# A fused attention and FFN kernel: down projections and one 128x128 product as three split products, the last layernorm's factor from VectorE

## Chip, cores and metric

The kernel runs on one core of a Trainium2 chip. The metric is the device time of one execution in microseconds (us), the median of several runs. The core has five engines that work side by side, each through its own instructions in order: TensorE (PE in the profile; PEld is its weight load), VectorE (DVE), ScalarE (ACT), GpSimd (POOL) and SyncE (SP, here only DMAs). They wait for each other through counting semaphores.

## What is computed

The input x has 4 batches of 2048 tokens with 256 features, all in fp32. The reference, cut to what matters:

```python
x = x + attn_a(layernorm(x))        # 16 heads of 16, linear attention
x = x + ffn(layernorm(x))
x = x + attn_b(layernorm(x))        # only the first 16 tokens of a batch differ from "+ ob"
x = x + ffn(layernorm(x))

# attn_a: feature map elu(.) + 1 on q and k
q, k, v = fm(x @ Wq + bq), fm(x @ Wk + bk), x @ Wv + bv
kv  = einsum('bkhd,bkhm->bhdm', k, v)
out = einsum('bqhd,bhdm->bqhm', q, kv) / max(einsum('bqhd,bkhd->bqh', q, k), 1e-6)
out = out.reshape(B, S, D) @ Wo + bo

# ffn: square(relu(x @ Ws1)) @ Ws2 + routed experts, whose weights are truncated to 0 or 1
```

The routed experts count only where a token's second logit reaches its first; the kernel tests a bound on that once and skips them, as in these runs. The third sublayer adds the row ob to all tokens except the first 16 of each batch, 64 in all, which get a chain of small products of their own.

## The kernel before

The tokens are worked in 16 groups of 512 (4 tiles of 128 tokens). All of x and all q stay in SBUF.

The first pass, 0 to about 180 us, makes k, q and the sums k^T x for each group; the change leaves its instructions alone. Its products q and k are split already: a matrix is written as hi + lo, where hi is the value rounded to the type float32r (a copy by ScalarE) and lo the rounded rest (a subtraction), and a product is hi*hi + hi*lo + lo*hi, three matmuls in that type, summed in PSUM.

The second pass is a loop over steps i = 0 to 17, three stages deep. Step i works on group i for attention, on group r = i - 1 for the first FFN (F1, F2), and on group v = i - 2 for the last FFN's down projection (F4). The order on each engine is that of its `step` function, written by hand:

- TensorE: transposes of x for group r (L1367, into PA); the attention product of group i (L1377, into PT and PB), which waits until VectorE has emptied PB (L998); `down(PA)` for group v (L1356); slot 1; the up product for group r (L1395, into PT); transposes of o_tok (L1403, into PB); four transposes that spread ln_rsq of the second layernorm over the partitions, called r2 (L1408, into PT); slot 2; the output product W of group i, three split products (L1425, L1426, L1431); the product of h2s with wc (L1435), which adds to the up product; slot 3; `down(PB)` for group r (L1356).
- ScalarE: copies the transposes of x (L688), scales half of F4's result (L695), rounds o to o_hi (L702), then relu (L706) and square (L708) of h2, and behind L1435 relu (L714) and square (L716) of h3.
- VectorE: quotients (L945, L949) and o_tok (L953), half of F4's result (L969), slot 1, o_lo (L977), h2s = h2 times the spread factor (L984), slot 2, adds W to x (L990), statistics (L934), adds F2 to x (L998), slot 3, statistics (L934) for the last layernorm.
- GpSimd: `rsq`, once for each of the two layernorms: five small instructions for the variance (L454 to L461) and a power -1 (L463), then adds the row ob to x (L429), slot 1, adds y3, the half of F4's result that ScalarE scaled (L517), slot 2.

The scale enters the FFN as relu(x*w)^2 times rstd^2, so the factor is 1/variance (times a constant that is folded in). wc is ws2 times w1c, so that the last FFN's hidden layer comes from the same PSUM bank. The slots hold the pieces of the chain for the 64 tokens (`chain(i, slot)`), different in each step. The down projections, the product with wc and the up product are plain fp32 matmuls, two instructions each on TensorE.

Of the kernel before, what the change touches and what calls it, by code (L numbers as in the profile page):

```python
# [44 lines left out]
def hybrid_kernel(nc, x_in, Wq, bq, Wk, bk, Wv, bv, Wo, bo, qw, qb, kw, vw, vb, ow, ob,  # L45
# [18 lines left out]
    with ExitStack() as ctx:  # L64
# [78 lines left out]
        squares = o_tok.rearrange("p k n -> p (k n)").rearrange("p (c n) -> p c n", c=C)  # L143


        with ExitStack() as pass1_memory:
            def sb1(name, shape):
                return pass1_memory.enter_context(nc.sbuf_tensor(name, shape, F32R))

            wq_hi, wq_lo = sb1("wq_hi", [P, C, D]), sb1("wq_lo", [P, C, D])  # L150
            wk_hi, wk_lo = sb1("wk_hi", [P, C, D]), sb1("wk_lo", [P, C, D])
            xt_hi, xt_lo = sb1("xt_hi", [P, C, GT]), sb1("xt_lo", [P, C, GT])
# [107 lines left out]
        (c_wts, c_vecs, c_xs, c_out, c_blk, c_bd, c_bd_sb, c_brow, c_brow_sb, c_fold, c_fold_sb, c_stat, c_rstd, c_z, c_zt, c_zt_sb,  # L260
         c_qkv, c_lin, c_k, c_vi, c_ss, c_rs, c_lt, c_q1, c_kn, c_knt, c_knm, c_vsel, c_vm, c_logit, c_lg, c_pr, c_pt, c_p1,
         c_inv, c_pv, c_o, c_ot, c_ot_sb, c_ql, c_dsum, c_diff, c_flag, c_proj, c_hid, c_relu, c_sq, c_ffn, c_added, c_final, c_zero,
         c_pool) = [sem(f"c_{n}") for n in (
             "wts", "vecs", "xs", "out", "blk", "bd", "bd_sb", "brow", "brow_sb", "fold", "fold_sb", "stat", "rstd", "z", "zt", "zt_sb",
             "qkv", "lin", "k", "vi", "ss", "rs", "lt", "q1", "kn", "knt", "knm", "vsel", "vm", "logit", "lg", "pr", "pt", "p1",
             "inv", "pv", "o", "ot", "ot_sb", "ql", "dsum", "diff", "flag", "proj", "hid", "relu", "sq", "ffn", "added", "final", "zero",
             "pool")]

# [1332 lines left out]
```

## Time and profile before

| | |
|---|---|
| median of 3 runs | 457.89 us (457.2 to 458.69) |
| profiled execution | 457.29 us, of it span 455.5 us |
| mean granted TensorE clock | 0.993 |
| busy: PE | 425.2 us (93%) |
| busy: DVE | 293.2 us (64%) |
| busy: ACT | 183.8 us (40%) |
| busy: POOL | 203.5 us (45%) |
| chain that ended last | PE 82%, DVE 7%, ACT 5%, POOL 2% |
| from 194 to 443 us | PE 238.8 of 249 us busy, DVE 185.7, ACT 90.9, POOL 132.6 |

The span reaches from the first to the last instruction; the profiled execution's time has 1.8 us around it. "Busy" counts the time in which an engine works on an instruction. Matmuls overlap each other, so a matmul's own duration is longer than the distance from one to the next. The chain follows the work that ended last back from the end, at each step to what it waited for. Line numbers are those of the kernel before; a helper's line stands for all its calls.

### The profile page before, as it was taken

What the parts mean: (1) busy time and instruction counts of PE and PEld (TensorE: products, weight loads), DVE (VectorE), ACT (ScalarE), POOL (GpSimd) and SP (SyncE); (2) the same over time, 40 slices, a digit from 0 to 9 for tenths busy, and PEclk for the clock granted to TensorE, in tenths of its full rate; (3) what the DMA queues carried; (4) which work ended last, traced back from release to release, by engine and by line L of the source; (5) the groups of instructions that cost most, each with busy time, mean ns of one, the idle gap of its engine ahead of it and who ended that gap; (6) DMA issues with size and microseconds to landing.
All of it is one profiled execution on the core that took longest, in us unless ns stands there. A gap on an engine that the chain in (4) does not pass through costs nothing.

```text
span 455.5 us, 7618 instructions
## 1 busy us (share of the span) xinstructions
PE 425.2 (93%) x2570; PEld 354.7 (78%) x2570; DVE 293.2 (64%) x651; ACT 183.8 (40%) x321; POOL 203.5 (45%) x334
## 2 busy tenths in 40 slices
PE   7799989999999999688979999999999999999971
PEld 4689979998898999676858876878777787787851
DVE  4565575455556543459637697878858777887843
ACT  2464545555455541224134532333243323424440
POOL 3344442433334350036144367566527527635562
PEclk9999999999999999999999999999999999999997
DMA  8512111111100003100110111011010111011102
GB/s 260 179 48 78 63 47 46 48 46 46 46 0 1 0 2 89 8 2 3 51 46 4 50 49 35 15 48 47 4 47 1 50 48 35 16 49 47 48 32 71
DMA packets 22776, 20.58 MB, mean 45 GB/s; under 512 B 3255, under 2 KB 22717, under 8 KB 22717
## 3 DMA queue, kind: packets, MB, share of 16 engines
q1 hardware_dynamic: 22156, 19.32, 13.5%
q8 instruction: 30, 0.49, 0.4%
q10 hardware_dynamic: 560, 0.52, 0.4%
q14 instruction: 30, 0.24, 0.2%
HBM read 11.32 MB, written 8.45 MB: 43 GB/s over the span
## 4 chain that ended last, share of the span: by engine, by line
PE 82%; DVE 7%; ACT 5%; issue 2%; POOL 2%; DMA 1%; POOLq 0%; ACTq 0%; DVEq 0%
PE PG L1236 11%; PE PB L1356 6%; PE PT L1395 6%; PE PA L1356 5%; PE PB L1377 5%; PE PA L1425 4%; PE PA L1431 3%; PE PA L1426 3%; PE PA L1226 3%; PE PA L1227 3%; PE PA L1228 3%; PE PB L1214 3%; PE PB L1212 3%; PE PB L1213 3%; PE PT L1435 3%; PE PA L1367 3%
## 5 line engine op out<-in xcount | busy, mean ns | idle before, releaser
L454 POOL TENSOR_TENSOR ln_a<-ln_bn 128x4 f32<-128x4 f32 x32 | 6.5, 205 | 132.0 <-DVE ln_bn L934 132.0
L1236 PE MATMUL PG<-scratch 128*128 128x256 f32 x256 | 58.0, 379 | 1.3 <-DVE scratch L821 1.3
L821 DVE SCALAR_TENSOR_TENSOR scratch<-scratch,PB 128x1024 f32<-128x1024 f32 x16 | 19.5, 1221 | 60.3 <-ACT scratch L570 60.3
L1236 PEld LDWEIGHTS PG<-scratch 128*128 128x128 f32 x256 | 47.4, 190 | 7.4 <-issue 1.5
L535 ACT ACTIVATE scratch<-x_all,ln_shift,ln_rstd 128x255 f32 (+1 forms) x60 | 31.1, 589 | 36.7 <-PE PG L1236 30.2
L934 DVE BATCH_NORM_STATS2 ln_bn<-x_all 128x6 f32<-128x256 f32 x128 | 44.9, 413 | 0.9
L416 POOL TENSOR_SCALAR ln_rstd<-ln_mv 128x4 f32<-128x4 f32 x16 | 3.7, 228 | 91.3 <-DVE ln_mv L743 88.4
L1212 PE MATMUL PB<-wk_hi,xt_hi 128*128 128x256 f32 x128 | 39.0, 305 | 0.4 <-DVE xt_lo L768 0.4
L429 POOL TENSOR_TENSOR x_all<-x_all,scratch 128x1024 f32 (+1 forms) x16 | 38.2, 2388 | 0.6 <-ACT scratch L535 0.5
L429 POOL TENSOR_TENSOR x_all<-x_all,ob_rows 128x1024 f32<-128x1024 f32 x16 | 37.8, 2360 | 0.0
L695 ACT ACTIVATE scratch<-PA,ln_rsq 128x256 f32<-128x256 f32 x32 | 13.4, 471 | 59.3 <-PE PA L1356 35.4
L1425 PE MATMUL PA<-wo_hi,o_hi 128*128 128x256 f32 x128 | 33.5, 295 | 3.1 <-ACT o_hi L702 2.7
L1214 PE MATMUL PB<-wk_hi,xt_lo 128*128 128x256 f32 x128 | 36.2, 282 | 0.0
L1213 PE MATMUL PB<-wk_lo,xt_hi 128*128 128x256 f32 x128 | 36.1, 282 | 0.0
L463 POOL TENSOR_TENSOR ln_rsq<-ln_a,minus_ones 128x4 f32<-128x4 f32 x32 | 32.5, 1015 | 2.5
L1356 PE MATMUL PA<-ws,scratch 128*128 128x256 f32 x128 | 30.4, 380 | 2.7 <-ACT scratch L688 2.7
L990 DVE TENSOR_TENSOR x_all<-PA,x_all 128x1024 f32<-128x1024 f32 x16 | 19.6, 1225 | 20.6 <-PE PA L1431 20.6
L977 DVE TENSOR_TENSOR o_lo<-PB,o_hi 128x512 fp32r<-128x512 f32 x32 | 20.6, 684 | 18.6 <-ACT o_hi L702 18.5
L1426 PE MATMUL PA<-wo_lo,o_hi 128*128 128x256 f32 x128 | 31.9, 282 | 0.0
L1356 PE MATMUL PB<-ws,scratch 128*128 128x256 f32 x128 | 31.1, 386 | 0.0
L1395 PE MATMUL PT<-scratch 128*128 128x512 f32 x64 | 30.9, 605 | 0.0
L576 ACT ACTIVATE scratch<-PA,minus_one 128x1024 f32<-128x1024 f32 x16 | 17.8, 1115 | 30.2 <-PE PA L1228 28.9
(239 smaller groups left out, 1039.0 us busy)
## 6 DMA issues: line engine op xcount, KB each, us to landing
out_dram<-x_all SPq DMA_DIRECT2D x16, 512.0 KB, 3.1
x_all<-n_L_attn_a_inputs_q_dram SPq DMA_DIRECT2D x15, 512.0 KB, 3.6
x_all<-n_L_attn_a_inputs_q_dram ACTq DMA_DIRECT2D x2, 128.0 KB, 2.8
x_all<-n_L_attn_a_inputs_q_dram SPq DMA_DIRECT2D x2, 128.0 KB, 2.6
scratch<-in_L_attn_a_Wk_dram SPq DMA_DIRECT2D x1, 256.0 KB, 4.6
scratch<-in_L_attn_a_Wq_dram ACTq DMA_DIRECT2D x1, 256.0 KB, 5.0
scratch<-in_L_attn_a_Wv_dram SPq DMA_DIRECT2D x1, 256.0 KB, 6.8
scratch<-in_L_attn_a_Wo_dram SPq DMA_DIRECT2D x1, 256.0 KB, 6.2
```

What stands on the lines that cost most here:

```text
L429: nc.gpsimd.tensor_tensor(x_group(n), x_group(n), rows_[:, :].rearrange("p (o d) -> p o d", o=1).to_broadcast([P, T, D]), ALU.add).then_in ...
L463: nc.gpsimd.tensor_tensor(ln_rsq[:, slot, :], a, minus_ones[:, :], ALU.pow).then_inc(done, 1)
L535: nc.scalar.activation(dst[:, t:t + 1, 0:width], x_tile(n, t)[:, :, 0:width], ACT.Identity, scale=ln_rstd[:, slot, t:t + 1], bias=ln_shift ...
L934: nc.vector.bn_stats(ln_bn[:, slot, t:t + 1, :], x_tile(n, t)).then_inc(bn, 1)
L1212: mm(dst, hi, wk_hi[:, c, :], start=(c == 0), stop=False)
L1213: mm(dst, hi, wk_lo[:, c, :], start=False, stop=False)
L1214: last = mm(dst, lo, wk_hi[:, c, :], start=False, stop=(c == C - 1))
L1236: last = mm(PG[:, c, 0:D], k_tok[:, t, c * P:(c + 1) * P], xn[g % 2][:, t, :], start=(g == 0 and t == 0), stop=(g == G - 1 and t == T - 1))
L1356: last = mm(four(pair)[:, t, :], h[:, t * P:(t + 1) * P], ws2[:, :], start=True, stop=True)
L1395: last = mm(PT[:, 0, :], w1c[:, c, :], x2t[:, c, :], start=(c == 0), stop=(c == C - 1))
L1425: mm(four(PA)[:, t, :], hi, wo_hi[:, c, :], start=(c == 0), stop=False)
L1426: mm(four(PA)[:, t, :], hi, wo_lo[:, c, :], start=False, stop=False)
```

## The change

Four parts:

1. `down` takes hi and lo of the hidden layer and of ws2 and makes three matmuls for each tile of 128 tokens. The product with wc becomes three matmuls of 512 columns; the third, with h2_lo, has a wait of its own. ws2 and wc are split once, in `fold_ffn` (ScalarE) and in step 0 (VectorE).
2. For this the hidden layers are needed as hi and lo. ScalarE squares twice, first into h2_hi (h3_hi), rounded, then in place; GpSimd subtracts (`h2_low`, `h3_low`). The factor now multiplies before the square, so it is 1/sqrt(variance) (power -0.5, in `half_rstd2`) and h2 stands for what h2s was.
3. The last layernorm's factor is VectorE's reciprocal (`reciprocal_variances`), placed after the quotients and ahead of the writes of o_tok; GpSimd makes only the variances (`four_variances`). VectorE's statistics for it stand ahead of slot 3.
4. Buffers lie elsewhere in SBUF; several semaphores of the chain for the 64 tokens are joined into three that count on (c_once, c_made, c_taken).

```diff
-            def rsq(slot, j, bn, powed, done):
+            def four_variances(slot, j, bn, powed):
...
-                nc.gpsimd.tensor_tensor(ln_rsq[:, slot, :], a, minus_ones[:, :], ALU.pow).then_inc(done, 1)
+            def half_rstd2(r):
+                ge(pool, r2_mm, r)
+                four_variances(0, r, bn2, pow2)
+                pool.wait_ge(pow2, 5 * r + 5)
+                nc.gpsimd.tensor_tensor(ln_rsq[:, 0, :], ln_a[:, 0, :], minus_half[:, 0:T], ALU.pow).then_inc(rsq2, 1)
+            def h2_low(r):
+                pool.wait_ge(f1_sq, r + 1)
+                ge(pool, f2_mm, r)
+                nc.gpsimd.tensor_tensor(h2_lo[:, :], h2, h2_hi[:, :].bitcast(F32), ALU.subtract).then_inc(h2_lo_done, 1)
+            def h3_low(v):
+                pool.wait_ge(f3_sq, v + 1)
+                ge(pool, f4_mm, v)
+                nc.gpsimd.tensor_tensor(h3_lo[:, :], h3, h3_hi[:, :].bitcast(F32), ALU.subtract).then_inc(h3_lo_done, 1)
...
 # ScalarE, step
-                    ge(act, f1_scaled, r)
+                    ge(act, h2_lo_done, r)
                     nc.scalar.activation(h2, PT[:, 0, :], ACT.Relu, scale=2.0).then_inc(f1_relu, 1)
-                    act.wait_ge(f1_relu, r + 1)
+                    act.wait_ge(f1_scaled, r + 1)
+                    ge(act, f2_mm, r)
+                    nc.scalar.activation(h2_hi[:, :], h2, ACT.Square).then_inc(h2_hi_done, 1)
+                    act.wait_ge(h2_hi_done, r + 1)
                     nc.scalar.activation(h2, h2, ACT.Square).then_inc(f1_sq, 1)
...
 # VectorE, step
+            def reciprocal_variances(v):
+                dve.wait_ge(pow3, 5 * (v + 1))
+                ge(dve, f4_scaled, 2 * v)
+                nc.vector.reciprocal(ln_rsq[:, 1, :], ln_a[:, 1, :]).then_inc(rsq3, 1)
...
                     nc.vector.reciprocal(norm_inv[:, :, :], norm_sb[:, :, :]).then_inc(o_norm, 1)
+                    if runs(v):
+                        reciprocal_variances(v)
...
-                    dve.wait_ge(f1_sq, r + 1)
+                    dve.wait_ge(f1_relu, r + 1)
                     dve.wait_ge(r2_mm, r + 1)
-                    nc.vector.tensor_tensor(h2s, h2, PT[:, 1, :], ALU.mult).then_inc(f1_scaled, 1)
+                    nc.vector.tensor_tensor(h2, h2, PT[:, 1, :], ALU.mult).then_inc(f1_scaled, 1)
...
 # TensorE
-            def down(pair, h, done):
+            def down(pair, hi, lo, done):
                 for t in range(T):
-                    last = mm(four(pair)[:, t, :], h[:, t * P:(t + 1) * P], ws2[:, :], start=True, stop=True)
+                    dst, tile = four(pair)[:, t, :], slice(t * P, (t + 1) * P)
+                    mm(dst, hi[:, tile], ws2_hi[:, :], start=True, stop=False)
+                    mm(dst, hi[:, tile], ws2_lo[:, :], start=False, stop=False)
+                    last = mm(dst, lo[:, tile], ws2_hi[:, :], start=False, stop=True)
...
-                    pe.wait_ge(f1_scaled, r + 1)
-                    mm(PT[:, 0, :], wc, h2s, start=False, stop=True, skip_group_check=True).then_inc(f3_mm, 1)
+                    pe.wait_ge(h2_hi_done, r + 1)
+                    mm(PT[:, 0, :], wc_hi[:, :], h2_hi[:, :], start=False, stop=False, skip_group_check=True)
+                    mm(PT[:, 0, :], wc_lo[:, :], h2_hi[:, :], start=False, stop=False, skip_group_check=True)
+                    pe.wait_ge(h2_lo_done, r + 1)
+                    mm(PT[:, 0, :], wc_hi[:, :], h2_lo[:, :], start=False, stop=True, skip_group_check=True).then_inc(f3_mm, 1)
```

GpSimd's queue in step 15, before; first the variance and power of the second layernorm (waiting for bn2; only its last row stands here), then those of the last (bn3).

```order
L463 TENSOR_TENSOR ln_rsq<-ln_a,minus_ones 128x4 [waits pow2]
L454 TENSOR_TENSOR ln_a<-ln_bn 128x4 [waits bn3,f4_scaled,out_dve]
L455 TENSOR_TENSOR ln_d<-ln_bn 128x4
L457 TENSOR_SCALAR ln_a<-ln_a 128x4 [waits pow3]
L459 TENSOR_TENSOR ln_d<-ln_d 128x4 [waits pow3]
L461 TENSOR_TENSOR ln_a<-ln_a,ln_d 128x4 [waits pow3]
L463 TENSOR_TENSOR ln_rsq<-ln_a,minus_ones 128x4 [waits pow3]
L429 TENSOR_TENSOR x_all<-x_all,ob_rows 128x1024 [waits t2_mm]
L517 TENSOR_TENSOR x_all<-x_all,scratch 128x512 [waits f4_scaled]
```

GpSimd's queue in step 15, now; h_lo is h2_lo or h3_lo, scratch beside h_hi is h2 or h3.

```order
L498 TENSOR_TENSOR h_lo<-scratch,h_hi 128x512 [waits f4_mm,f3_sq]
L475 TENSOR_TENSOR ln_a<-ln_bn 128x4 [waits bn2,r2_mm]
...
L488 TENSOR_TENSOR ln_rsq<-ln_a,minus_half 128x4 [waits pow2]
L475 TENSOR_TENSOR ln_a<-ln_bn 128x4 [waits bn3,rsq3]
L476 TENSOR_TENSOR ln_d<-ln_bn 128x4
L478 TENSOR_SCALAR ln_a<-ln_a 128x4 [waits pow3]
L480 TENSOR_TENSOR ln_d<-ln_d 128x4 [waits pow3]
L482 TENSOR_TENSOR ln_a<-ln_a,ln_d 128x4 [waits pow3]
L450 TENSOR_TENSOR x_all<-x_all,ob_rows 128x1024 [waits t2_mm]
L551 TENSOR_TENSOR x_all<-x_all,scratch 128x512 [waits f4_scaled]
L493 TENSOR_TENSOR h_lo<-scratch,h_hi 128x512 [waits f2_mm,f1_sq]
```

A subtraction stands at the head of the step and another at its end, ahead of what slots 1 and 2 hold in other steps; the second power is gone.

TensorE's queue in step 15 from the up product to the output product, before.

```order
L1395 MATMUL PT<-scratch 128x512 [waits t2_done]
L1403 MATMUL PB<-ident,scratch 128x128 [waits o_done]
L1403 MATMUL PB<-ident,scratch 128x128 x7
L1408 MATMUL PT<-ident,ln_rsq 128x128 [waits rsq2]
L1408 MATMUL PT<-ident,ln_rsq 128x128 x3
L1443 MATMUL PG<-ident,b_weights 128x64 [waits c_z]
L1443 MATMUL PG<-ident,b_weights 128x64
L1425 MATMUL PA<-wo_hi,o_hi 128x256 [waits f4_scaled,out_dve,o_hi_done]
```

The same stretch now.

```order
L1456 MATMUL PT<-scratch,ffn_weights 128x512 [waits t2_done]
L1463 MATMUL PT<-ident,ln_rsq 128x128 [waits o_done,rsq2]
L1463 MATMUL PT<-ident,ln_rsq 128x128 x3
L1471 MATMUL PB<-ident,scratch 128x128 [waits o_done]
L1471 MATMUL PB<-ident,scratch 128x128 x7
L1509 MATMUL PG<-ident,b_weights 128x64 [waits c_z]
L1509 MATMUL PG<-ident,b_weights 128x64
L1488 MATMUL PA<-wo_hi,o_hi 128x256 [waits f4_scaled,out_dve,o_hi_done]
```

The transposes of the factor (r2) stand ahead of those of o_tok and wait for the first write of o_tok besides, since that write frees their bank.

## Rows read from the trace of the kernel before

**Rows 1.** The chain of waits, 416 to 431 us: start, us, what.
```profile
416.61 0.86 PE PT L1435 x2
...
422.17 1.73 PE PA L1356 x8
...
423.90 1.72 PE PT L1395 x4
...
426.15 0.40 ACT o_hi L702
...
426.64 0.60 ACT o_hi L702
...
427.90 0.12 PE PA L1426
```

**Rows 2.** TensorE's timeline: start, us, line, out<-in; last matmuls of W, and L1435.
```profile
192.08 0.64 PE L1431 MATMUL PA<-wo_hi,o_lo 128*128 128x256 f32 x4
...
416.45 1.02 PE L1435 MATMUL PT<-scratch 128*128 128x512 f32 x2
...
430.25 1.02 PE L1435 MATMUL PT<-scratch 128*128 128x512 f32 x2
```

**Rows 3.** ScalarE's timeline in step 15.
```profile
417.51 0.69 ACT L714 ACTIVATE scratch<-PT,w1ob 128x512 f32<-128x512 f32 x1 [3.50 <-PE PT L1435]
...
418.23 0.63 ACT L716 ACTIVATE scratch<-scratch 128x512 f32<-128x512 f32 x1
...
426.15 1.08 ACT L702 ACTIVATE o_hi<-PB 128x512 fp32r<-128x512 f32 x2 [0.87 <-PE PB L1403]
...
427.12 0.61 ACT L706 ACTIVATE scratch<-PT 128x512 f32<-128x512 f32 x1
```

**Rows 4.** TensorE's timeline in the first pass: split products of 512 columns.
```profile
174.31 0.40 PE L1227 MATMUL PA<-xt_lo,wq_hi 128*128 128x512 f32 x1
...
174.55 0.39 PE L1228 MATMUL PA<-xt_hi,wq_lo 128*128 128x512 f32 x1
```

**Rows 5.** GpSimd's timeline in step 15.
```profile
422.07 0.20 POOL L454 TENSOR_TENSOR ln_a<-ln_bn 128x4 f32<-128x4 f32 x1 [0.31 <-DVE ln_bn L934]
...
423.34 1.01 POOL L463 TENSOR_TENSOR ln_rsq<-ln_a,minus_ones 128x4 f32<-128x4 f32 x1
...
424.32 2.36 POOL L429 TENSOR_TENSOR x_all<-x_all,ob_rows 128x1024 f32<-128x1024 f32 x1
...
426.64 1.33 POOL L517 TENSOR_TENSOR x_all<-x_all,scratch 128x512 f32<-128x512 f32 x1
```

**Rows 6.** VectorE's timeline in step 15.
```profile
422.60 0.55 DVE L949 RECIPROCAL norm_inv<-norm_sb 128x64 f32<-128x64 f32 x1
...
423.19 0.42 DVE L953 TENSOR_TENSOR scratch<-PT,norm_inv 128x256 f32<-128x256 f32 x1
...
424.46 0.88 DVE L969 SCALAR_TENSOR_TENSOR x_all<-PA,ln_rsq,x_all 128x256 f32<-128x256 f32 x2
...
425.25 1.57 DVE L1145 TENSOR_SCALAR b_weights<-q_all 64x256 f32<-64x256 f32 x1
...
426.78 1.29 DVE L977 TENSOR_TENSOR o_lo<-PB,o_hi 128x512 fp32r<-128x512 f32 x2
...
428.43 0.69 DVE L984 TENSOR_TENSOR scratch<-scratch,PT 128x512 f32<-128x512 f32 x1 [0.36 <-ACT scratch L708]
```

**Rows 7.** Step 5: VectorE's zz (L1070), then GpSimd's power for it.
```profile
269.31 1.18 DVE L1070 TENSOR_SCALAR b_weights<-q_all 64x256 f32<-64x256 f32 x1
...
267.96 0.55 POOL L478 TENSOR_TENSOR q_all<-q_all,minus_half 64x1 f32<-64x1 f32 x1
```

**Rows 8.** Step 7: VectorE's L1082 and L1083, then GpSimd's addition beside them.
```profile
296.64 1.69 DVE L1082 TENSOR_TENSOR q_all<-q_all,b_weights 64x256 f32<-64x256 f32 x1
...
298.36 0.42 DVE L1083 TENSOR_TENSOR q_all<-q_all 64x256 f32<-64x256 f32 x1
...
295.70 2.35 POOL L429 TENSOR_TENSOR x_all<-x_all,ob_rows 128x1024 f32<-128x1024 f32 x1
```

More of the change, by code:

```diff
@@ L138, in hybrid_kernel @@
+        wc_hi, wc_lo = sb("wc_hi", [P, F], F32R), sb("wc_lo", [P, F], F32R)
+        ws2_hi, ws2_lo = sb("ws2_hi", [P, D], F32R), sb("ws2_lo", [P, D], F32R)
+        h2_hi, h2_lo = sb("h2_hi", [P, GT], F32R), sb("h2_lo", [P, GT], F32R)
+        h3_hi, h3_lo = sb("h3_hi", [P, GT], F32R), sb("h3_lo", [P, GT], F32R)
+        part = parts(sb("ffn_weights", [P, 2560])[:, :])
         w1c = part(C * F).rearrange("p (c f) -> p c f", c=C)
@@ L142, in hybrid_kernel @@
         ob_t = part(C * P).rearrange("p (c n) -> p c n", c=C)
[L143 to L152, printed above, removed]
+        h2s = h2
         b_weights = sb("b_weights", [P, 2, 4, C * D])
@@ L259, in hybrid_kernel @@
         c_link = sem("c_link")
[L260 to L267, printed above, removed]
+        c_wts, c_vecs, c_xs, c_out, c_blk, c_bd, c_brow, c_fold, c_fold_sb, c_stat = [sem(f"c_{n}") for n in (
+            "wts", "vecs", "xs", "out", "blk", "bd", "brow", "fold", "fold_sb", "stat")]
+        c_rstd, c_z, c_zt, c_zt_sb, c_lin, c_ss, c_rs, c_lt, c_q1, c_knm = [sem(f"c_{n}") for n in (
+            "rstd", "z", "zt", "zt_sb", "lin", "ss", "rs", "lt", "q1", "knm")]
+        c_vm, c_logit, c_lg, c_pr, c_pt, c_p1, c_inv, c_pv, c_o, c_ot = [sem(f"c_{n}") for n in (
+            "vm", "logit", "lg", "pr", "pt", "p1", "inv", "pv", "o", "ot")]
+        c_ot_sb, c_ql, c_zero, c_pool, c_once, c_made, c_taken = [sem(f"c_{n}") for n in (
+            "ot_sb", "ql", "zero", "pool", "once", "made", "taken")]
+        QKV, VSEL, KNT, DIFF, PROJ, HID, FFN = range(1, 8)
+        K, VI, KN, DSUM, FLAG, ADDED, FINAL = range(1, 8)
         waits_passed = {"sp": sem("sp_waits_passed"), "act": sem("act_waits_passed"),
@@ L517, in step @@
                     nc.gpsimd.tensor_tensor(last, last, y3, ALU.add).then_inc(out_pool, 1)
+                if runs(r):
+                    h2_low(r)
+                chain(i, 1)
                 chain(i, 2)
@@ L1396, in step @@
                     last.then_inc(f1_mm, 1)
+                if runs(r):
+                    pe.wait_ge(rsq2, r + 1)
+                    if runs(i):
+                        pe.wait_ge(o_done, 3 * i + 1)
+                    for t in range(T):
+                        last = nc.tensor.transpose(PT[:, 1, t * P:(t + 1) * P], ln_rsq[:, 0, t:t + 1].to_broadcast([P, P]), ident[:, :])
+                    last.then_inc(r2_mm, 1)
                 if i == 0:
```

186 lines of the change are left out of this document (103 added, 83 removed).

## Prediction, made before the changed kernel was run

> **What bounds the kernel now.** I read the chain of waits first, then each engine's timeline for one step. The change touches only the second pass (the loop over i, from 194 us to the end), so the question is what sets the period of that loop. In the chain for step 15, the lightest full step, TensorE follows on TensorE almost everywhere: the product with wc (L1435) 0.86 us, down(PA) 1.73, the up product (L1395) 1.72 [rows 1]. ScalarE appears once, with 0.40 + 0.60 us of o_hi ahead of the output product, since that starts only when both halves are rounded. W is the name here for that output product (24 matmuls of 0.12 us), and "W end" the start of L1435 behind it. Step 15 runs from the W end at 416.45 to 430.25, 13.8 us; over the 15 intervals that start at 192.56 (where the last matmul of W for i = 0 leaves 0.48 us after 192.08) and end at 430.25, a period is 15.8 us on average [rows 1, 2]. The rest of the 15.8 is the small chain for 64 tokens, laid into slots 1, 2 and 3 of a step.
>
> The other three engines have gaps: ScalarE waits 3.5 us for L1435 before L714 [rows 3], and GpSimd and VectorE wait for each other in turn. I looked at these gaps because every term that the change adds goes into them, and a gap covers only what is ready when it comes.
>
> **What TensorE saves.** A full fp32 product with 256 columns takes two instructions and 0.43 us (1.73 / 4). A split one takes 0.12, so three take 0.36 and a down projection 1.44: 0.29 less. The 512-column split product has a pitch of 0.23 (174.31 to 174.55) [rows 4], three take 0.69 against 0.86: 0.17 less. In total 32 x 0.29 + 16 x 0.17 = 12.0 us of TensorE time.
>
> **What is added.** ScalarE squares twice (0.63 more, 32 times, as L716) [rows 3]. GpSimd makes both low parts: a 128x512 subtraction of two SBUF operands, which L517 shows at 1.33 [rows 5]; the addition of twice as many elements goes on to the next after 2.32 (424.32 to 426.64), 1.16 for this size. Between the two I take 1.25, 32 times. GpSimd loses one of two powers (1.01) per step; VectorE gets a reciprocal of four elements per partition. The trace has no such row: above stands the 0.55 of 64 elements (L949), below nothing at all; I take 0.17, as most of 0.55 should go with the elements [rows 6]. At the fold ScalarE makes two more copies, two of 256 and 128 columns; a rounding of 512 takes 0.5 [rows 3], so both together between 0.3 and 0.8, and I take 0.5, ahead of o_hi for i = 0; VectorE's two differences lie beside them.
>
> **What moves.** The weighting with the factor now stands between relu and square, so h2_hi needs ScalarE, VectorE, ScalarE in turn (before: ScalarE twice, then VectorE), as long as before. But the third product with wc waits for h2_lo, behind a second square and GpSimd: 0.63 + 1.25 us later. GpSimd starts a step with h3_lo, and that waits for ScalarE's last square; behind it are queued the powers for factor 2 and the variances for factor 3. On VectorE the reciprocal stands ahead of the three writes of o_tok, so o_tok, and with it the whole attention path, now waits for that GpSimd queue. TensorE has r2 ahead of the transposes of o_tok, so these 0.53 us no longer cover ScalarE's o_hi.
>
> **One step replayed.** I lay the durations of the rows one behind another for step 15, t = 0 at W end, 0.2 us from TensorE to another engine and 0.05 otherwise (both read off starts against ends in the rows). h2_lo is done at 1.04, the third product ends at 1.26. ScalarE: relu 1.5 to 2.2, h3_hi to 2.8, square to 3.45 [rows 3]. GpSimd: h3_lo 3.5 to 4.75, factor 2 (2.28, from 422.07 to the power's end) to 7.0, variances of factor 3 (1.27, from 422.07 to 423.34) to 8.3 [rows 5]. VectorE: reciprocal 8.55, o_tok (1.27 from 423.19 to 424.46) to 9.8 [rows 6]. VectorE was ready at 6.8, so 1.5 us are waited. TensorE: first half of the transposes 10.27; ScalarE: o_hi 10.5 to 11.6, relu to 12.2. VectorE: slot 1 (1.55 us in this step) to 12.15, o_lo twice to 13.4, weighting to 14.05; ScalarE h2_hi to 14.7, square to 15.35; GpSimd h2_lo to 16.65; the third product ends at 16.9. W ends at 15.4, so the two matmuls with h2_hi are over by 15.9 and 0.8 us are bare.
>
> This is a closed ring: from third product to third product 16.9 - 1.26 = 15.7 us here, and 14.4 in a step without slot 1, of which TensorE has under 1.5. Before there was no such ring: f4 needed only the first square, o_tok only the quotients. So step 15 goes from 13.8 to 15.4 at W end. What TensorE saves inside a ring that it does not set is worth nothing.
>
> **All steps.** The same laying out for the code before, with the slots' items from the trace, gives 11.6, 16.3, 21.0, 15.2, 14.4, 16.8, 15.7, 15.6, 15.9, 14.6, 17.4, 15.1, 17.8, 14.7, 13.9 for the intervals 1 to 15; the trace has 11.7, 15.7, 21.4, 15.1, 14.2, 17.2, 15.9, 15.7, 16.4, 14.8, 17.8, 15.2, 17.9, 14.8, 13.8 (the first starts and the last ends in [rows 2]). With the new order: 11.6, 18.1, 21.0, 15.6, 16.2, 19.9, 17.4, 17.7, 15.9, 15.9, 17.6, 15.4, 18.1, 14.8, 15.4. The differences are of three kinds. Intervals 2, 5, 7, 8, 10 and 15 have the ring bare: together +10.2. Intervals 1, 3, 4, 9 and 11 to 14 have so much TensorE work in their slots that it covers the ring: +1.3 together. Interval 6 has +3.1: GpSimd's slot 1 stood ahead of its y3 addition and now stands behind h2_lo, and in step 5 VectorE's zz (L1070) waits for that slot's power. It ended at 268.5, before zz started at 269.31 [rows 7]; now it ends about 2.0 after W end, zz takes 1.18, and only then come the sum of W and the statistics behind it on VectorE, while TensorE's slot 3 waits for zz ahead of down(PB).
>
> That is 14.6 us. The drain adds 0.9: both low parts and a second square are bare there (the last power, 1.02, goes). The fold adds 0.5. Sum 16.0 us. The profiled execution took 457.29 (span 455.5 and 1.8 around it), 0.6 below the median of 457.89; 457.3 + 16.0 = **473.3 us**. Layout, semaphores and the first pass I cost at nothing: no instruction or transfer there changes its form or its wait.
>
> **A port.** VectorE's L1082 takes 1.69 us, while L1083 behind it, with as many elements, takes 0.42; GpSimd's addition runs from 295.70 to 298.05, and L1082 ends at 298.33 [rows 8]. So some VectorE operations stand still while GpSimd reads memory. The Trainium skill (SBUF — State Buffer, "SBUF: two separate sides") states it as a lock: an operation of VectorE with two SBUF inputs and one of GpSimd that reads SBUF exclude each other for the whole instruction. By that rule the 32 new subtractions can also stop such items of the 64-token chain; the operations of the ring itself read PSUM on one side, and the trace agrees that they keep their time beside GpSimd (L969 0.88 for two, beside the addition at 424.32 [rows 5, 6]).
>
> **Rivals.**
> (a) TensorE stays the bound, as in [rows 1], and its 12.0 us come back: 445 us. For it: 93% busy, and it is the chain in nearly every row. Against it: GpSimd's queue of h3_lo, factor 2, variances ends at 8.3, and VectorE's o_tok stood at 6.8. It would decide if those finished 1.5 us earlier. Chance 0.06.
> (b) The ring is there but loses its overhang, because h_lo is shorter than L517 (1.0 in place of 1.25): the same laying out then gives 5.5 less, 468; if it took 0.65, about 459 to 461. Below half of L517 no row speaks for it. This is in my range; a result within 0.3% of before, 0.03.
> (c) The port. About five steps have two-SBUF items in slot 2 or 3 just where h2_lo now runs, each can lose up to 1.26, with some slack: +2 to +6, or h_lo itself is held up and takes 1.6 (+8): 476 to 482. Chance 0.14.
> (d) Only step 5's wait and the moved r2 cost, the rest is covered: 3.1 for step 5 and 16 x 0.4 for what r2 covered, less a third of the 12.0: 463. For it: TensorE's slots hide the ring in eight intervals already. Against it: VectorE's 1.5 us of waiting in the light step. Chance 0.07.
> (e) The change doesn't do what it says (the split products not at the pitch of 0.12): then TensorE gets longer, not shorter, and the time is at the upper end. Chance 0.01.
> My forecast, 466 to 476, has 0.69.
>
> **How the numbers follow.** What a measurement here can tell from no change is about 0.3%, 1.4 us. Faster 0.06, same 0.03, slower 0.91. The range 461 to 483 holds (b), (c) and (d), leaving out (a) and the far ends; the likeliest case's own is 466 to 476.
>
> **What would show it.** In the new profile: 12 us less busy TensorE time, but its share of the span falls from 93% to about 88%; a wait of the third product with wc for GpSimd's h_lo, about 0.6 us in light steps; VectorE's reciprocal waiting for ln_a, 1.5 us or more in most steps; W waiting 0.9 for o_hi; zz waiting about 3 in step 5. If the reciprocal doesn't wait, the ring is wrong; if h_lo isn't 1.2 to 1.3 us, its size is.

## The result and the profile after

The changed kernel takes 469.77 us (467.0 to 473.73, 4 runs) against 458.29 us for the kernel before on the same chip (457.2 to 458.75, 4 runs): ratio 1.0261 [1.0181, 1.0341], so slower by 2.6%. The same kernel run again with the experiments gave 470.47. The profiled execution took 470.83, its span 469.1: 13.6 us more than the span before.

The page of the changed kernel (busy us, share of the span, number of instructions; then the granted clock in 40 slices; then the chain that ended last):

```profile
PE 424.2 (90%) x2714; PEld 361.1 (77%) x2714; DVE 288.2 (61%) x669; ACT 203.8 (43%) x355; POOL 227.7 (49%) x350
...
PEclk8999999999999999999999989999999999999995
...
PE 50%; issue 16%; POOL 16%; DVE 13%; ACT 3%; DMA 1%; POOLq 0%; DVEq 0%; SPq 0%; ACTq 0%
```

TensorE had 82% of the chain, GpSimd 2%. Now they have 50% and 16%: the end is set by a loop through the engines.

The waits of the changed kernel from 205 to 470 us (who waited, for what: us in total, times, longest):

```profile
POOL h_lo L493 <- ACT scratch L750: 60.9, 16, 7.6
...
DVE ln_rsq L984 <- POOL ln_a L482: 17.0, 12, 2.3
...
PE PT L1501 <- POOL h_lo L493: 8.9, 13, 1.3
...
PE PA L1488 <- ACT o_hi L741: 5.8, 9, 0.8
...
DVE b_weights L1127 <- POOL q_all L513: 3.6, 1, 3.6
```

Line by line: GpSimd waits for ScalarE's second square before it can make h2_lo; VectorE's new reciprocal waits for GpSimd's variances 12 times; TensorE's third product with wc waits for GpSimd's h2_lo 13 times, its output product W for o_hi 9 times; and one item of the 64-token chain, zz, waits 3.6 us once. Before, W waited for o_hi too, but 1.4 us in 4 times, and VectorE waited for GpSimd's power, but behind its writes of o_tok, so that the attention path did not (kernel before, 205 us to the end):

```profile
DVE x_all L969 <- POOL ln_rsq L463: 6.6, 7, 2.6
```

Step 15 of the changed kernel, to be laid beside [rows 1, 3, 5, 6]. TensorE's timeline (start, duration, line; in brackets the idle time before it and what ended it):

```profile
427.42 0.40 PE L1498 MATMUL PT<-h_hi,wc_hi 128*128 128x512 f32 x1
...
428.43 0.50 PE L1501 MATMUL PT<-h_lo,wc_hi 128*128 128x512 f32 x1 [0.38 <-POOL h_lo L493]
428.77 0.28 PE L1414 MATMUL PB<-ws_hi,h_hi 128*128 128x256 f32 x1
...
430.21 1.03 PE L1427 MATMUL PA<-ident,x_all 128*128 128x128 f32 x8
...
439.17 0.38 PE L1488 MATMUL PA<-wo_hi,o_hi 128*128 128x256 f32 x1 [0.46 <-ACT o_hi L741]
...
442.14 0.40 PE L1498 MATMUL PT<-h_hi,wc_hi 128*128 128x512 f32 x1
...
443.29 0.50 PE L1501 MATMUL PT<-h_lo,wc_hi 128*128 128x512 f32 x1 [0.51 <-POOL h_lo L493]
```

GpSimd's timeline there:

```profile
431.06 1.27 POOL L498 TENSOR_TENSOR h_lo<-scratch,h_hi 128x512 fp32r<-128x512 f32 x1 [1.83 <-ACT scratch L761]
...
433.58 1.02 POOL L488 TENSOR_TENSOR ln_rsq<-ln_a,minus_half 128x4 f32<-128x4 f32 x1
...
435.56 0.20 POOL L482 TENSOR_TENSOR ln_a<-ln_a,ln_d 128x4 f32<-128x4 f32 x1
435.71 2.36 POOL L450 TENSOR_TENSOR x_all<-x_all,ob_rows 128x1024 f32<-128x1024 f32 x1
...
441.96 1.27 POOL L493 TENSOR_TENSOR h_lo<-scratch,h_hi 128x512 fp32r<-128x512 f32 x1 [2.50 <-ACT scratch L750]
```

VectorE's timeline there:

```profile
435.80 0.18 DVE L984 RECIPROCAL ln_rsq<-ln_a 128x4 f32<-128x4 f32 x1 [1.48 <-POOL ln_a L482]
435.89 0.41 DVE L1005 TENSOR_TENSOR scratch<-PT,norm_inv 128x256 f32<-128x256 f32 x1
...
437.93 0.40 DVE L1202 TENSOR_SCALAR b_weights<-q_all 64x256 f32<-64x256 f32 x1
438.67 1.29 DVE L1034 TENSOR_TENSOR o_lo<-PB,o_hi 128x512 fp32r<-128x512 f32 x2 [0.34 <-ACT o_hi L741]
```

Read in a circle, each piece waiting for the one before it: third product 428.43, h3_lo 431.06, factor 2 to 434.6, variances of factor 3 to 435.76, reciprocal 435.80, o_tok, o_hi, the weighting, two squares, h2_lo 441.96, third product 443.29. This circle is called the ring below. One round takes 443.29 - 428.43 = 14.9 us, and the W ends (the starts of L1498) are 442.14 - 427.42 = 14.7 apart, 13.8 before [rows 2].

The same reading for every interval between W ends, in us (interval 15 is the one just read; intervals are those of the prediction), gives where the 13.6 us are:

| interval | 2 | 3 | 4 | 5 | 6 | 7 | 8 | 9 | 10 | 11 | 12 | 13 | 14 | 15 |
|---|---|---|---|---|---|---|---|---|---|---|---|---|---|---|
| before | 15.7 | 21.3 | 15.1 | 14.2 | 17.2 | 15.9 | 15.7 | 16.4 | 14.8 | 17.8 | 15.2 | 17.9 | 14.8 | 13.8 |
| after | 16.3 | 22.0 | 15.6 | 14.9 | 20.5 | 16.7 | 17.7 | 16.0 | 15.8 | 18.3 | 15.1 | 18.3 | 14.5 | 14.7 |

They add up to 10.5 more. The start of L1498 for interval 1 is 1.4 later (205.68 against 204.26); the stretch from the last W end in the table to the end takes 27.0 against 25.2, 1.7 more (from the unrounded starts).

### The profile page after: what moved, and what is told of

Same layout as the page of the kernel before. It is cut to its first block, busy times and chain, and to the rows that moved or that the text cites. A ratio compares the mean times of both kernels' runs of the same rounds, so it can differ in the third digit from the quotient of the medians.

```text
span 469.1 us, 8063 instructions
## 1 busy us (share of the span) xinstructions
PE 424.2 (90%) x2714; PEld 361.1 (77%) x2714; DVE 288.2 (61%) x669; ACT 203.8 (43%) x355; POOL 227.7 (49%) x350
## 4 chain that ended last, share of the span: by engine, by line
PE 50%; issue 16%; POOL 16%; DVE 13%; ACT 3%; DMA 1%; POOLq 0%; DVEq 0%; SPq 0%; ACTq 0%
PE PG L1293 11%; PE PA L1283 3%; PE PA L1284 3%; PE PA L1285 3%; PE PB L1271 3%; PE PB L1269 3%; PE PB L1270 3%; POOL h_lo L493 3%; PE PT L1225 2%; DVE ln_bn L979 2%; POOL ln_rsq L488 2%; POOL x_all L450 2%; POOL h_lo L498 2%; PE PB L1437 2%; POOL x_all L551 2%
## 5 line engine op out<-in xcount | busy, mean ns | idle before, releaser
L493 POOL TENSOR_TENSOR h_lo<-scratch,h_hi 128x512 fp32r<-128x512 f32 x16 | 20.5, 1281 | 60.9 <-ACT scratch L750 60.9
L450 POOL TENSOR_TENSOR x_all<-x_all,wvo 128x1024 f32 (+1 forms) x16 | 38.2, 2390 | 0.6 <-ACT scratch L572 0.5
L498 POOL TENSOR_TENSOR h_lo<-scratch,h_hi 128x512 fp32r<-128x512 f32 x16 | 20.4, 1275 | 31.0 <-ACT scratch L761 31.0
L1488 PEld LDWEIGHTS PA<-wo_hi,o_hi 128*128 128x128 f32 x128 | 24.3, 190 | 10.6 <-ACT o_hi L741 10.1
L741 ACT ACTIVATE o_hi<-PB 128x512 fp32r<-128x512 f32 x32 | 17.4, 595 | 33.0 <-PE PB L1471 33.0
L1054 DVE TENSOR_TENSOR x_all<-PB,x_all 128x1024 f32<-128x1024 f32 x16 | 19.6, 1224 | 19.1 <-PE PB L1416 19.0
L613 ACT ACTIVATE scratch<-PA,minus_one 128x1024 f32<-128x1024 f32 x16 | 17.8, 1115 | 30.2 <-PE PA L1285 28.9
L1456 PE MATMUL PT<-scratch,ffn_weights 128*128 128x512 f32 x64 | 30.9, 605 | 0.0
```

The source lines that it names most:

```text
L450: nc.gpsimd.tensor_tensor(x_group(n), x_group(n), rows_[:, :].rearrange("p (o d) -> p o d", o=1).to_broadcast([P, T, D]), ALU.add).then_in ...
L493: nc.gpsimd.tensor_tensor(h2_lo[:, :], h2, h2_hi[:, :].bitcast(F32), ALU.subtract).then_inc(h2_lo_done, 1)
L498: nc.gpsimd.tensor_tensor(h3_lo[:, :], h3, h3_hi[:, :].bitcast(F32), ALU.subtract).then_inc(h3_lo_done, 1)
L1456: last = mm(PT[:, 0, :], w1c[:, c, :], x2t[:, c, :], start=(c == 0), stop=(c == C - 1))
L1488: mm(four(PA)[:, t, :], hi, wo_hi[:, c, :], start=(c == 0), stop=False)
```

## The experiments

"The changed kernel" is here the run that follows; each time is a median, each ratio against the kernel before in the same job (457.28 us in the first, 457.18 in the second, 457.92 in the third).

**The changed kernel again.** No edit.

> The changed kernel once more, unaltered, as the measure for the kernels beside it. Both theories: 467 to 474 us, the kernel before near 458.

Measured: 470.47 us (468.19 to 473.22), ratio 1.0269 [1.0232, 1.0306]. The slowdown stands, and this is the base of the comparisons. The interval around it is about 1.7 us wide on either side, because the executions differ in the clock granted to TensorE (see the last section); differences of 3 to 4 us are read with that in mind.

**The reciprocal behind o_tok** takes the wait for GpSimd's variances out of the attention path.

```diff
                     nc.vector.reciprocal(norm_inv[:, :, :], norm_sb[:, :, :]).then_inc(o_norm, 1)
-                    if runs(v):
-                        reciprocal_variances(v)
                     dve.wait_ge(o_norm, 2 * i + 2)
 ...
-                elif runs(v):
+                if runs(v):
                     reciprocal_variances(v)
```

> VectorE's reciprocal stands behind the three writes of o_tok instead of ahead of them; nothing else is altered. Ring theory (the time is set by a closed chain h2_lo, third product, relu, squares, h3_lo, factor 2, variances, reciprocal, o_tok, o_hi, and round to h2_lo): o_tok no longer waits for GpSimd, about 1 us less in the light steps, 5 to 7 us less in all. Rival (the low parts as such cost: TensorE stands bare for h_lo, 0.4 to 0.9 us in most steps, and the place of the reciprocal is covered): no more than 1 us less.

Measured: 467.13 us (466.67 to 467.16), ratio 1.0209 [1.0192, 1.0227]: 3.3 less. The waits of this kernel:

```profile
PE PT L1499 <- POOL h_lo L493: 9.2, 14, 1.3
...
PE PA L1486 <- ACT o_hi L741: 5.3, 8, 0.8
DVE ln_rsq L984 <- POOL ln_a L482: 5.2, 5, 2.3
```

The reciprocal's own waits fall from 17.0 us to 5.2, so the edit did what it should, but TensorE waits for h_lo and o_hi just as long as before it. The gain lies between the 5 to 7 of my theory and the rival's 1, so neither is right as it stands. The trace shows where the rest went. The slot item of step 15, which takes 0.40 in the changed kernel, is here early enough to run beside GpSimd's addition, and takes 1.35:

```profile
433.71 1.35 DVE L1200 TENSOR_SCALAR b_weights<-q_all 64x256 f32<-64x256 f32 x1
```

```profile
432.55 2.36 POOL L450 TENSOR_TENSOR x_all<-x_all,ob_rows 128x1024 f32<-128x1024 f32 x1
```

Items in intervals 2, 5 and 7 grow by 1.1 us each in the same way, and these three intervals get shorter by 0.1 at most; 8, 10 and 15 do by 1.1, 0.7 and 0.6, the last although its item grew. Summed over the second pass VectorE's items of the 64-token chain take 31.3 us here, against 27.1 in the changed kernel. So this run does not say how much of the ring the reciprocal's wait is.

**h2_lo on VectorE** behind slot 2, not on GpSimd.

```diff
 # GpSimd
-                if runs(r):
-                    h2_low(r)
                 chain(i, 1)
 # VectorE, behind slot 2
+                if runs(r):
+                    dve.wait_ge(f1_sq, r + 1)
+                    ge(dve, f2_mm, r)
+                    nc.vector.tensor_tensor(h2_lo[:, :], h2, h2_hi[:, :].bitcast(F32), ALU.subtract).then_inc(h2_lo_done, 1)
```

> h2_lo is subtracted by VectorE, behind slot 2 and ahead of the sum of W, instead of by GpSimd. Ring theory: 0.6 us less from the second square to the third product, and step 5's wait of VectorE for GpSimd (3.6 us in the trace) goes: 9 to 12 us less, near 459. Rival (VectorE is the engine without room in this pass, 0.6 us more for it in each of 16 steps): no gain or up to 5 us more.

Measured: 457.23 us (456.44 to 460.19, 10 runs), ratio 1.0003 [0.998, 1.0025]: 13.2 less, and the slowdown is gone. VectorE's rows, and its wait and TensorE's:

```profile
430.42 0.69 DVE L1038 TENSOR_TENSOR h_lo<-scratch,h_hi 128x512 fp32r<-128x512 f32 x1 [1.36 <-ACT scratch L743]
```

```profile
DVE ln_rsq L977 <- POOL ln_a L482: 14.0, 13, 2.3
...
PE PT L1498 <- DVE h_lo L1038: 1.1, 3, 0.7
```

The subtraction takes 0.69 us on VectorE against 1.27 on GpSimd, 0.58 less. In the profiled executions intervals 2, 3, 5, 10, 11, 13 and 15 fall by 0.6 to 0.7 each, 4 and 7 by 0.2 and 0.5, and 9, 12 and 14 not at all. Interval 6, with the wait of zz at step 5's end, falls from 20.5 to 17.3, and interval 8, where GpSimd's powers for the 64 tokens stand behind h2_lo in the changed kernel, from 17.7 to 15.6. The edit takes h2_lo out of GpSimd's queue as well, so it removes two things at once. TensorE's wait for h_lo falls from 8.9 us to 1.1, while the reciprocal still waits 14.0: of the two places it is h2_lo that sets the time.

**The subtraction twice on GpSimd**, the second one signals.

```diff
-                nc.gpsimd.tensor_tensor(h2_lo[:, :], h2, h2_hi[:, :].bitcast(F32), ALU.subtract).then_inc(h2_lo_done, 1)
+                nc.gpsimd.tensor_tensor(h2_lo[:, :], h2, h2_hi[:, :].bitcast(F32), ALU.subtract).then_inc(h2_lo_first, 1)
+                pool.wait_ge(h2_lo_first, r + 1)
+                nc.gpsimd.tensor_tensor(h2_lo[:, :], h2, h2_hi[:, :].bitcast(F32), ALU.subtract).then_inc(h2_lo_done, 1)
```

> GpSimd makes the subtraction for h2_lo twice, the second signals: 1.3 us more, 16 times, same result. Ring theory: nearly all of it is on the path in every step but those with much TensorE work in slots, 14 to 20 us more. Rival (TensorE's work sets the time, GpSimd has room at 49% busy): 0 to 4 us more.

Measured: 494.55 us (494.02 to 498.73), ratio 1.0843 [1.0792, 1.0893]: 24 more, above the 14 to 20 of my theory. TensorE's wait in this kernel:

```profile
PE PT L1504 <- POOL h_lo L496: 28.9, 16, 2.6
```

It is 20.0 us longer than in the changed kernel (8.9), nearly 16 times the 1.27 added. The intervals say the same: all are 0.9 to 1.4 us longer, the heavy ones too, except 6 and 13 with 2.1 and 3.0. The granted clock was 0.958 to 0.971 here, against 0.976 to 0.989 for the changed kernel in the same job, and the profiled execution has four slices in the second pass below 9 tenths (24, 27, 34 and 39):

```profile
PEclk9999999999999999999999979989999998999985
```

Two of these slices lie in intervals 6 and 13. The other 4 us go with the lower clock, but I did not separate them.

**GpSimd's slot 1 ahead of h2_lo**, as it stood before.

```diff
+                chain(i, 1)
                 if runs(r):
                     h2_low(r)
-                chain(i, 1)
                 chain(i, 2)
```

> GpSimd's slot 1 stands ahead of h2_low, as it stood ahead of the y3 addition before; nothing else is altered. Ring theory: the step 5 wait of VectorE for GpSimd (3.6 us) goes and GpSimd's powers for the 64 tokens no longer hold h3_lo back: 3 to 4 us less than the changed kernel. Rival (that wait is covered by other work): 0 to 1 us less.

Measured: 467.27 us (465.09 to 469.85), ratio 1.0204 [1.016, 1.0249]: 3.2 less, as expected, though the intervals of the two ratios overlap a little. In the profiled executions interval 6 falls by 2.6 us and interval 8 by 1.1, where GpSimd's powers no longer hold h3_lo back; no other gets shorter by more than 0.03. zz in step 5 stands at 276.56 in VectorE's timeline, with no wait in front of it:

```profile
276.56 0.40 DVE L1127 TENSOR_SCALAR b_weights<-q_all 64x256 f32<-64x256 f32 x1
```

**The down projections in full fp32**, with both low parts still made and waited for. ScalarE's relu here also has to wait until TensorE has read the hidden layer of the step before (not shown); in the trace it never does wait for that.

```diff
-            def down(pair, hi, lo, done):
+            def down(pair, h, done):
                 for t in range(T):
-                    ...three split products...
+                    last = mm(four(pair)[:, t, :], h[:, t * P:(t + 1) * P], ws2[:, :], start=True, stop=True)
```

> The down projections are full fp32 products again (two instructions a tile, of h2, h3 and ws2), while the low parts are still made and waited for; the product with wc stays split. TensorE gets 32 x 0.29 = 9.3 us more work than in the changed kernel. Ring theory: most of that work lies beside the ring and covers itself, 3 to 5 us more than the changed kernel (by the same laying out of rows, 3.7), 472 to 476. Rival (what TensorE saves is worth its full length): 9 us more, 479.

Measured: 474.49 us (472.9 to 475.12), ratio 1.0383 [1.0366, 1.04]: 4.0 more by the medians, 5.2 by the ratios. Against executions of the changed kernel with the same mean granted clock (0.989 and 0.993) it is about 6. So of the 32 x 0.29 = 9.3 us that the split saves TensorE, 4 to 6 are worth something here. The intervals show where: 2, 5, 10 and 15, the light ones, are the same to 0.03 us although TensorE works longer in them, while 3, 4, 9, 11 and 12 take 0.4 to 0.6 more. That is what a ring through the other engines predicts.

**The kernel before with the reciprocal alone.**

```diff
-                nc.gpsimd.tensor_tensor(ln_rsq[:, slot, :], a, minus_ones[:, :], ALU.pow).then_inc(done, 1)
+                if power:
+                    pool.wait_ge(powed, 5 * j + 5)
+                    nc.gpsimd.tensor_tensor(ln_rsq[:, slot, :], a, minus_ones[:, :], ALU.pow).then_inc(done, 1)
 # VectorE, behind the quotients
+                    if runs(v):
+                        reciprocal_variances(v)
```

> The kernel before with one part of the change alone: the last layernorm's factor by VectorE's reciprocal, ahead of the writes of o_tok, without any low part. Ring theory: GpSimd's queue ends before VectorE has the quotients, so the reciprocal waits for nothing: within 1.5 us of the kernel before. Rival (the reciprocal's place is what made the changed kernel slow): 5 us or more above the kernel before.

Measured: 454.42 us (454.3 to 456.05), ratio 0.9942 [0.992, 0.9965]: faster by 2.8, about twice what I had allowed. The reciprocal starts at once in step 15, where it had waited 1.48 us in the changed kernel. I had expected it to wait for nothing anywhere, but it still waits 7 times, 5.4 us in all:

```profile
421.50 0.18 DVE L939 RECIPROCAL ln_rsq<-ln_a 128x4 f32<-128x4 f32 x1
```

```profile
DVE ln_rsq L939 <- POOL ln_a L461: 5.4, 7, 1.4
```

Interval 2 falls by 1.1, from 15.7 to 14.55, interval 5 by 0.4, and the stretch behind the last L1435 from 13.7 to 12.9. Interval 2 has the first items of the 64-token chain (three, L1054 in the kernel before), and they take 1.76 us here, 2.99 before. This part of the change is good by itself. Of the 17.0 us that the reciprocal waits in the changed kernel, 5.4 are there without any low part; the rest came with h3_lo, queued ahead of the variances on GpSimd, and with the new order, which I did not separate.

**Three edits at once:** h2_lo on VectorE, the reciprocal behind o_tok, and r2 behind the transposes of o_tok, so that it covers o_hi again.

```diff
 # beside the edits of the two kernels above; TensorE:
                         last.then_inc(ot_mm, 1)
+                if runs(r):
+                    pe.wait_ge(rsq2, r + 1)
+                    for t in range(T):
+                        last = nc.tensor.transpose(PT[:, 1, t * P:(t + 1) * P], ln_rsq[:, 0, t:t + 1].to_broadcast([P, P]), ident[:, :])
+                    last.then_inc(r2_mm, 1)
```

> The changed kernel with h2_lo on VectorE, the reciprocal behind the writes of o_tok, and TensorE's four transposes of the factor behind those of o_tok, as before. Ring theory: the ring is shorter than TensorE's work in nearly all steps, so part of the 12 us saved comes out at last: 452 to 456 us. Rival (h2_lo on VectorE took away all that could be had, the rest is covered): 457, as with that alone.

Measured: 452.91 us (452.53 to 453.73), ratio 0.9912 [0.9895, 0.9929]: faster than both kernels, by 4.3 and 17.6 us. Its waits:

```profile
DVE ln_rsq L977 <- POOL ln_a L482: 3.6, 2, 2.3
...
PE PA L1481 <- ACT o_hi L734: 1.4, 4, 0.4
...
PE PT L1494 <- DVE h_lo L1036: 0.9, 2, 0.7
```

The three new waits on the attention path and at the third product are nearly gone; o_hi is back at the 1.4 us of the kernel before. But the kernel before with the reciprocal alone took 454.42 in the same job. All the split products together, with their low parts in the best places found, are worth 1.5 us over that, and the intervals of the two ratios overlap.

**That version with the down projections in full fp32.** The edit is that of the run with the down projections above.

> The version with h2_lo on VectorE, the reciprocal behind o_tok and r2 behind the transposes of o_tok (452.9 us), with the down projections as full fp32 products again (the low parts are still made and waited for). My theory: once the ring is open, TensorE sets the period again, so what the split saves there comes back in full: a down projection takes 1.52 us from start to next start in that version's trace at 417.14 (12 products) against 1.73, so 32 x 0.21 = 6.7 us, up to 32 x 0.29 = 9.3: 459.5 to 462. Rival: something other than TensorE still sets most steps, and the saving is worth no more than the 4.0 us of the same edit in the changed kernel: 456 to 457.5.

Measured: 461.57 us (459.4 to 462.12, 9 runs), ratio 1.0061 [1.004, 1.0083]: 8.7 more by the medians, 6.8 by the ratios (1.0061 - 0.9912, of 457.5). The rival's 4.0 (456 to 457.5) is out. With the ring open TensorE sets the period in most intervals, and most of its saving comes back: intervals 2 to 15 take 6.5 us more together, though 2 and 5 still take nothing. What comes back is measured against a kernel that makes the low parts and does not use them; it is not what the split is worth as a whole.

**That version with down(PA) alone in full fp32** and no split of h3 at all.

```diff
 # GpSimd
-                if runs(v):
-                    h3_low(v)
 # TensorE
-                    down(PA, h3_hi, h3_lo, f4_mm)
+                    down_full(PA, h3, f4_mm)
```

> The same version with only down(PA) as full fp32 product and no high or low part of h3 at all: GpSimd starts a step with factor 2, 1.3 us earlier, ScalarE has one square less, TensorE 16 x 0.21 to 0.29 = 3.4 to 4.6 us more. My theory (TensorE sets the period): 456 to 457.5. Rival: GpSimd's queue of h3_lo, factor 2 and variances still sets the steps, and without its first piece the time falls: 452 or less.

Measured: 456.21 us (455.43 to 457.27, 12 runs), ratio 0.9967 [0.9951, 0.9982]: 3.3 more (2.5 by the ratios), as my theory had it, although GpSimd has a piece of 1.27 us less in each step. Its queue no longer sets the steps.

## Why the prediction was right, and where it was off

The forecast was 473.3 us, the range 461 to 483, slower with 0.91; it is slower, at 469.8. The direction and the mechanism were right. That the size came so near is in part luck: the forecast added 16.0 us and had no term for the clock, while the changed kernel's median is 11.5 above the kernel before and its execution at the highest granted clock, 0.993, only 8.7. Step by step:

- **TensorE's saving: nearly right.** down(PB) at 428.77 has 1.44 us to the next instruction (430.21), as worked out; the product with wc takes 0.70 where nothing waits (419.52 to 420.22 in the last kernel but one above). down(PA), behind the attention product, takes 1.52 (433.10 to 434.62), so it saves 0.21 and not 0.29, and the 12.0 us are 10.7. But TensorE's busy time fell by 1 us, not 12 (425.2 to 424.2), and the share to 90%, not 88%. This sign was badly chosen: a lone split matmul is booked with 0.28 us at a pitch of 0.12, with 0.38 behind a wait (439.17), and with 0.41 at half clock. In the version with three edits, where these waits are nearly gone, busy time is 417.0. Pitch shows the saving, busy time hides it.
- **The closed ring: right, in form and place.** Reciprocal waiting for ln_a 1.48 (forecast 1.5), W for o_hi 0.46, with 0.33 of slot 2's transposes before it (forecast 0.9), third product bare 0.68 (443.29 - 442.38 - 0.23, where 442.38 is the second product's start; forecast 0.8). Up to the end of o_tok the replay is right to 0.05 us (9.81 after the W end at 427.42, forecast 9.8). The ring without slot 1 was forecast at 14.4 us and is 14.9: the slot's item of 0.40 is over 0.34 us before o_hi comes (438.67) and is not on it. Runs that made links of the ring longer or shorter moved the time the way they should, and the doubled subtraction in size too; only the one with the reciprocal behind o_tok leaves its size open.
- **h_lo and the reciprocal: right.** 1.27 to 1.28 us against 1.25, and 0.18 against 0.17.
- **Six bare intervals (2, 5, 7, 8, 10, 15): mis-sized.** Forecast +10.2, measured 0.6 + 0.7 + 0.8 + 2.0 + 1.0 + 0.9 = +6.0. This is the term that was mis-sized. In step 15 the sum took slot 1 at 1.55 us from L1145 [rows 6]; the same item now takes 0.40 (L1202). That time was no work of the item: before, it ended with GpSimd's addition (426.82 against 426.68). The moved order changed who stands beside it. So 15.7 was 1.3 too long for the slot and 0.5 too short for the ring itself. The three items of interval 2 (L1054) fell by 1.2, which is what that interval was over-forecast (1.8 against 0.6); L1066 in interval 5 fell by 1.3 (1.8 against 0.7). The run with the reciprocal behind o_tok bears this out: there the items of 2 and 5 grow again by 1.1, and these intervals gain next to nothing although the reciprocal no longer holds o_tok back. Interval 7 is not explained by it: L1082 fell by 1.3, but one item rose (L1083 to L1140, 0.42 to 1.38), so the two explain 0.3 of the 1.0 by which it was over-forecast. Intervals 8 and 10 were nearly right (2.1 and 1.3 forecast).
- **Covered intervals (3, 4, 9, 11 to 14): right as a sum.** Forecast +1.3 for eight, the seven in the table +1.2 (from the unrounded starts). One by one they are off by up to 0.7, in both directions.
- **Step 5: right number, two causes.** Forecast +3.1, interval 6 rose by 3.3, and putting slot 1 back took 2.6 off it. But only part of it is the wait itself. TensorE idles in front of zz's transposes, and then works at half clock (TensorE's timeline, changed kernel):

```profile
275.88 0.50 PE L1501 MATMUL PT<-h_lo,wc_hi 128*128 128x512 f32 x1 [0.75 <-POOL h_lo L493]
277.60 0.44 PE L1509 MATMUL PG<-ident,b_weights 64*128 64x64 f32 x2 [1.23 <-DVE b_weights L1127]
277.98 0.58 PE L1414 MATMUL PB<-ws_hi,h_hi 128*128 128x256 f32 x1
278.35 0.41 PE L1415 MATMUL PB<-ws_lo,h_hi 128*128 128x256 f32 x1
```

down(PB) takes 280.70 - 277.98 = 2.7 us there against 1.44: 1.3 of the 3.3. My replay had no slower clock and gave all 3.1 to waits, while waits make 2.0 of the measured 3.3; that the sum is right is luck. The run with the down projections in full fp32 has the same wait of 3.6 for zz and no fall of the clock there; its interval 6 is 19.8.
- **The fold: nothing.** 0.5 was taken. The 1.4 us at the first W end belong to the profiled execution, in which the clock granted in the first 12 us was 0.86 (the row stands under the next point), against 1.00 before; with the same fold, the run with the down projections in full fp32 has that start at 204.36, against 204.26 before.
- **The drain: too low.** Forecast +0.9, measured +1.7. Here is the changed kernel's last down(PB):

```profile
455.73 0.79 PE L1501 MATMUL PT<-h_lo,wc_hi 128*128 128x512 f32 x1 [1.27 <-POOL h_lo L493]
456.32 0.41 PE L1414 MATMUL PB<-ws_hi,h_hi 128*128 128x256 f32 x1
456.53 0.41 PE L1415 MATMUL PB<-ws_lo,h_hi 128*128 128x256 f32 x1
```

The pitch is 0.21 and not 0.12. The windows of the same kernel (stretch, length, busy time and count of PE, PEld, DVE, ACT and POOL, granted clock, DMA share, GB/s) say why:

```profile
0.00:12.00 12.00, 8.51 (x21) 5.07 (x22) 4.94 (x20) 2.91 (x4) 4.12 (x20) 0.86 0.87 259
...
457.00:469.00 12.00, 5.01 (x22) 4.42 (x21) 3.73 (x9) 2.35 (x5) 3.49 (x7) 0.50 0.16 51
```

The engine ran at 1.2 GHz there, behind gaps of 1.27 us and others; before, down(PB) stood at 442.75 and down(PA) at 444.48, 1.73 us apart as at the full clock. Two times 12 split matmuls at 0.21 in place of 0.12 are 2.2 us of TensorE's time. How much of it is on the path I did not test.

The terms as measured: 1.4 (start) + 10.5 (intervals: 6.0 + 1.2 + 3.3) + 1.7 (end) = 13.6 us. The forecast of 473.3 stands 2.5 above the profiled 470.8: 4.2 too much in the six intervals, 0.1 in the covered ones, 0.2 too little in interval 6, 0.9 at the start and 0.8 at the end. The start, and parts of step 5 and of the end, are the clock's and not the ring's: two errors, one each way, stand against each other. Of the rivals, (a) needed GpSimd's queue to be early, and it wasn't; (b) gave 468, nearer than the forecast, but its reason, a short h_lo, is refuted. (c), the port, has its sign turned round: the new order freed more items than it stopped (VectorE's items of the 64-token chain fell from 33.3 to 27.1 us in sum), and h_lo was not held up. (d) is refuted by the 12 waits of the reciprocal and the 13 of the third product, (e) by the pitch.

## What to carry to other kernels

A split product saves time on TensorE and puts a rounding and a subtraction on the path of its operand. Before splitting, close the loop from the product back to its operand through all engines, and compare its length with TensorE's work in a period; where they are near each other, the engine that makes the low part (0.69 us on VectorE, 1.27 on GpSimd, with a queue of other work behind it) decides between 457 and 470 us. Then compare with the kernel that has no split at all: here even the opened ring leaves 1.5 us of a saving of 10.7. And when an instruction's time includes standing still beside another engine, it is no constant: take it out of the sum wherever the change moves the neighbour.

## What was not expected of the hardware

**Slot items beside GpSimd.** In step 7 of the changed kernel VectorE has these rows, and GpSimd's addition L551 starts at 306.32 between them:

```profile
306.23 0.42 DVE L1139 TENSOR_TENSOR q_all<-q_all,b_weights 64x256 f32<-64x256 f32 x1
306.68 1.38 DVE L1140 TENSOR_TENSOR q_all<-q_all 64x256 f32<-64x256 f32 x1
```

```profile
306.32 1.46 POOL L551 TENSOR_TENSOR x_all<-x_all,scratch 128x512 f32<-128x512 f32 x1
```

L1139 had started first and keeps its 0.42, and the addition takes 1.46 in place of the 1.26 it takes in step 8 (at 323.92); L1140 comes behind it and stands still until it is over (307.78). Which one loses hangs on a tenth of a microsecond. The Trainium skill (SBUF — State Buffer, "SBUF: two separate sides") says that whichever of the two starts first keeps the shared port pair for the whole instruction; these rows agree. L1145 of the kernel before (1.57, and 0.40 as L1202 of the changed kernel) has a single 64x256 tensor and two columns of scalars as input, and was hit like those with two.

**The granted clock.** Executions of the changed kernel differ by 1.4%: 467.0 us at a mean clock of 0.993, 468.7 at 0.984, 470.8 at 0.978, 473.7 at 0.976. The kernel before stays at 0.989 to 0.996, and the version with three edits at 0.993 in all runs. The profiled execution shows where it falls (windows as above):

```profile
275.00:277.00 2.00, 0.62 (x2) 0.19 (x1) 0.23 (x1) 0.58 (x1) 1.83 (x4) 1.00 0.00 0
277.00:279.00 2.00, 1.40 (x7) 1.31 (x8) 1.97 (x4) 1.53 (x4) 0.81 (x2) 0.63 0.04 8
279.00:281.00 2.00, 2.00 (x11) 2.00 (x11) 1.09 (x5) 0.00 (x0) 1.45 (x5) 0.51 0.00 0
281.00:283.00 2.00, 2.00 (x18) 1.91 (x17) 1.97 (x4) 1.08 (x2) 1.32 (x3) 1.00 0.00 0
```

In the two us from 275 TensorE is busy for 0.62 only; then the clock goes to 0.5, the level of 1.2 GHz, and it is back at 281. This is slice 24 of the page. In the second execution with a profile the lowered slice is the 21st (from 236 us), in the run with slot 1 ahead it is the 21st too, and there the four us from 238 to 242 stand at 0.58 although TensorE is busy all the time:

```profile
232.00:238.00 6.00, 3.61 (x20) 3.37 (x21) 2.71 (x7) 2.07 (x6) 3.99 (x4) 0.71 0.00 0
238.00:242.00 4.00, 4.00 (x14) 2.80 (x14) 0.00 (x0) 0.00 (x0) 0.00 (x0) 0.58 0.38 131
```

So a wait on a path that was all TensorE before can be paid a second time, in the work behind it. The fall behind zz is in the second profiled execution too (281.7 to 285.4 us, interval 6 again 20.5), and in all is in four of the five traces that have this wait; where zz does not wait there is none. The fall at 236 to 242 us is in two traces and not in the first. The spread goes with these falls. Which gap brings one stays open. It is not the main cost: the execution at 0.993 is still 8.7 us slower than the kernel before.
